# Self-attention weights: the turning of each rounded 128x1024 unit moved from TensorE to a transposing DMA

## The reference, cut to what matters

```python
sim  = einsum('bhid,bhjd->bhij', fq(q, dq, 128., 8), fq(k, dk, 128., 8)) * SCALE
attn = softmax(sim, axis=-1)
out  = einsum('bhij,bhjd->bhid', fq(attn, dw, 0., 8), fq(v, dv, 128., 8))
# fq(x, delta, zp, 8): clip(round(x / delta) + zp, 0, 255) minus zp, times delta
```

## Time and profile before

| | |
|---|---|
| median of 3 runs | 3900.94 us |
| profiled execution | 3903.09 us |
| its span, first to last instruction | 3901.3 us |
| busy: PE, PEld | 3174.2, 2210.8 us |
| busy: DVE, ACT, POOL | 2174.1, 1624.8, 1328.8 us |
| mean granted TensorE clock | 0.872 |
| DMA queue of SyncE | 509.14 MB, 35.8% of 16 engines |

### The profile page before, as it was taken

How to read it: one execution, slowest core, us unless ns; L and a number is a source line. 1 busy time by engine, 2 the same in 40 slices (tenths; PEclk the granted TensorE clock), 3 DMA queues, 4 the chain that set the end, 5 groups by cost and what they waited for, 6 DMA issues and landing times.

```text
span 3901.3 us, 50803 instructions
## 1 busy us (share of the span) xinstructions
PE 3174.2 (81%) x19712; PEld 2210.8 (57%) x19712; DVE 2174.1 (56%) x3559; ACT 1624.8 (42%) x2666; POOL 1328.8 (34%) x1025
## 2 busy tenths in 40 slices
PE   4445658789968799989967799889977799989989
PEld 4334433445656555655756655655756555655767
DVE  2324538667455567467445557467455567467431
ACT  3312136447422267357422257346422267357421
POOL 1231326344331234244241234244231244244231
PEclk8677765669988889999988879989988899999999
DMA  6873543312343322322344322322343322322334
GB/s 211 287 279 154 191 172 130 130 54 77 130 150 138 133 105 77 140 103 82 150 136 150 132 76 76 141 98 77 131 151 142 133 98 76 141 108 77 133 127 173
DMA packets 227694, 514.00 MB, mean 132 GB/s; under 512 B 96512, under 2 KB 113152, under 8 KB 205440
## 3 DMA queue, kind: packets, MB, share of 16 engines
q1 hardware_dynamic: 215040, 509.14, 35.8%
q10 hardware_dynamic: 12416, 1.62, 0.3%
HBM read 428.39 MB, written 82.31 MB: 131 GB/s over the span
## 4 chain that ended last, share of the span: by engine, by line
PE 62%; DVE 13%; issue 7%; POOL 6%; ACT 5%; DMA 4%; SPq 2%; ACTq 1%; POOLq 0%; DVEq 0%
PE psum L1461 17%; PE psum L1462 15%; PE psum L1463 15%; PE psum L1734 6%; PE psum L1725 6%; DVE mx L1341 2%; PE psum L1748 2%; DVE stats L1233 1%; POOL w1b L791 1%; DMA kept<-st_lo 1%; DVE w1T L1360 1%; POOL rstd L749 1%; DVE x L1229 1%; DVE den L1347 1%; ACT e L1062 1%
## 5 line engine op out<-in xcount | busy, mean ns | idle before, releaser
L791 POOL TENSOR_SCALAR w1b<-e,rec 128x1024 f16<-128x1024 f32 x512 | 572.8, 1119 | 903.9 <-DVE rec L1349 751.0
L1341 DVE TENSOR_REDUCE mx<-psum 128x1 f32<-128x1024 f32 x512 | 625.5, 1222 | 326.6 <-PE psum L1725 323.0
L1062 ACT ACTIVATE e<-psum,nb,scale 128x1024 f32<-128x1024 f32 x512 | 616.6, 1204 | 16.7
L1461 PE MATMUL psum<-h_hi,fw_hi 128*128 128x512 f32 x1024 | 463.7, 453 | 2.1 <-DVE h_lo L1152 2.1
L1734 PEld LDWEIGHTS psum<-ident,w1b 128*128 128x128 f16 x4096 | 264.6, 106 | 329.7 <-issue 261.7
L1725 PE MATMUL psum<-k,q 32*128 32x512 bf16 x1024 | 355.6, 432 | 103.3 <-ACT e L1062 83.2
L1463 PE MATMUL psum<-h_hi,fw_lo 128*128 128x512 f32 x1024 | 422.1, 412 | 0.0
L1462 PE MATMUL psum<-h_lo,fw_hi 128*128 128x512 f32 x1024 | 421.3, 411 | 0.0
L1734 PE MATMUL psum<-ident,w1b 128*128 128x128 f16 x4096 | 356.7, 237 | 72.1 <-DVE w1T L1360 60.7
L1360 DVE TENSOR_SCALAR w1T<-psum 128x1024 bf16<-128x1024 f16 x512 | 347.1, 678 | 44.2 <-PE psum L1734 42.8
L1461 PE MATMUL psum<-w_hi,ht_hi 128*128 128x512 f32 x640 | 268.8, 420 | 74.2 <-DVE e L1287 39.4
(11 more groups left out here) (165 smaller groups left out, 5763.5 us busy)
## 6 DMA issues: line engine op xcount, KB each, us to landing
fw_hi<-pieces SPq DMA_DIRECT2D x192, 512.0 KB, 3.2
fw_lo<-pieces SPq DMA_DIRECT2D x192, 512.0 KB, 4.2
w_hi<-kept SPq DMA_DIRECT2D x80, 1024.0 KB, 4.9
w_lo<-kept SPq DMA_DIRECT2D x80, 1024.0 KB, 7.4
fbias<-in_fside_Bx16xSxS SPq DMA_DIRECT2D x64, 256.0 KB, 4.1
prep_raw<-in_L_xattn_ff_w SPq DMA_DIRECT2D x12, 1024.0 KB, 8.1
pieces<-prep_hi SPq DMA_DIRECT2D x24, 512.0 KB, 3.6
pieces<-prep_lo SPq DMA_DIRECT2D x24, 512.0 KB, 5.6
```

Of the source, the lines that this page charges most:

```text
L791: pool.tensor_scalar(w1b[u % NH][:], e1[u % NE][:], rec1[:, u % 8:u % 8 + 1], HALF, ALU.mult, ALU.add).then_inc(w1_ready.sem, 1)
L1062: act.activation(e1[s % NE][:], psum[:, i:i + 2, :].rearrange("p i n -> p (i n)"), ACT.Exp, bias=nb1[:, s % 4:s % 4 + 1], scale=scale[:, 0:1],
L1341: dve.tensor_reduce(mx1[:, s % 4:s % 4 + 1], psum[:, i:i + 2, :].rearrange("p i n -> p (i n)"), AX, ALU.max).then_inc(maxed1.sem, 1)
L1461: pe.matmul(o, s_hi, m_hi, start=first, stop=False)
```

## The change

Each unit's weights are no longer turned by TensorE through PSUM. VectorE now works before the turning: in slot s, on unit s-4, it waits for GpSimd's buffer and subtracts 1024 and clips at 255 in that buffer, in place, fp16 read and bf16 written over the same bytes. SyncE then waits for VectorE and issues one transposing DMA of the whole unit, 128x1024 two-byte elements, from w1b into w1T. TensorE's product waits for the four DMAs of its group. GpSimd refills a w1b buffer when its DMA has landed; there are four of them instead of three. Bank 4 is not used in this stage any more. In SyncE's program the DMA of unit s-4 stands ahead of everything else of slot s. The second cross attention keeps its way over TensorE.

```diff
-LAG_T = 5
+LAG_W, LAG_T = 4, 5
...
-            fills += [("p1T", n, u, 4) for u in range(UNITS)]
...
-        NE, NH = 5, 3
+        NE, NH = 5, 4
...
+        w1_whole = signal("w1_whole", units)
+        w1T_landed = [signal(f"w1T_landed{i}", [(n, u) for n, u in units if u % 8 == i], 16) for i in range(8)]
...
+            def turn_unit(n, u):
+
+                sp.wait_ge(w1_whole.sem, w1_whole.at((n, u)))
+                if u >= 8 and u % 4 == 0:
+                    g = u // 4 - 2
+                    if g % 4 == 3:
+                        wait_filled(sp, ("a1", n, g // 4))
+                    else:
+                        sp.wait_ge(w1T_used.sem, w1T_used.at((n, g)))
+                sp.dma_start_transpose(w1T[u % 8][:], w1b[u % NH][:].bitcast(BF16)).then_inc(w1T_landed[u % 8].sem, 16)
...
                 for s in range(S_SLOTS):
+                    if 0 <= s - LAG_W < UNITS:
+                        turn_unit(n, s - LAG_W)
...
                 if u >= NH:
-                    wait_filled(pool, ("p1T", n, u - NH))
+                    last = w1T_landed[(u - NH) % 8]
+                    pool.wait_ge(last.sem, last.at((n, u - NH)))
...
-                    u = s - LAG_T
+                    u = s - LAG_W
                     if 0 <= u < UNITS:
-                        key = ("p1T", n, u)
-                        wait_filled(dve, key)
...
-                        emptied_bank(dve.tensor_scalar(w1T[u % 8][:].rearrange("p k q -> p (k q)"),
-                                                       bank(bank_of(key)).bitcast(FP16), -HALF, W_HIGH, ALU.add, ALU.min), key)
+                        dve.wait_ge(w1_ready.sem, w1_ready.at((n, u)))
+                        dve.tensor_scalar(w1b[u % NH][:].bitcast(BF16), w1b[u % NH][:], -HALF, W_HIGH, ALU.add, ALU.min
+                                          ).then_inc(w1_whole.sem, 1)
...
-                    u = s - LAG_T
-                    if 0 <= u < UNITS:
-                        key = ("p1T", n, u)
-                        pe.wait_ge(w1_ready.sem, w1_ready.at((n, u)))
-                        wait_empty(key)
-                        for k in range(KEYT):
-                            ins = pe.transpose(bank(bank_of(key)).bitcast(FP16)[:, k * P:k * P + P],
-                                               w1b[u % NH][:, k * P:k * P + P], ident16[:])
-                        done(ins, key)
...
                         if part == 0:
-                            wait_emptied(pe, ("p1T", n, 4 * g + 3))
+                            for h in range(4):
+                                landed = w1T_landed[(4 * g + h) % 8]
+                                pe.wait_ge(landed.sem, landed.at((n, 4 * g + h)))
```

## The result

The change made the kernel slower: 4069.43 us median of four runs (4043.07 to 4079.38) against 3900.58 for the kernel before; ratio 1.0431, 95% interval 1.0393 to 1.0468. The profiled execution's span is 4061.1 us against 3901.3, the mean granted clock 0.799 against 0.872.

A forecast was written before the change was run, and what follows sets the result against it. TensorE sets the pace in seven of eight self-attention stages. Each: -34 + 34 + 5 + 3 = +8 us, seven +56; first stage +14, clock +28: +98, giving 4000 us. Forecast's own range 3910 to 4130, whole range 3800 to 4350.

The forecast's parts named there:

- Rival 1: Turning's landing as short as the shortest rows, 2.7 us; product waits under 1 us a group; 3770 us; chance 25%.
- rival 3: TensorE's clock falls in every group after waits of 3 us or more, a stage under 0.8; 4250 us; chance 12%.
- Removed, 34 us a stage: TensorE's eight transposes per unit and its bank wait go, saving 34 us in each of seven later stages, 238 us.
- VectorE's step, 0.43 us: In-place step in SBUF takes 0.43 us, from 678 ns out of PSUM, and may wait for a running GpSimd instruction.
- The new wait, 2.6 us in each of 13 groups a stage: TensorE stands 2.6 us before each product group for the DMA, landing taken as 4.5 us: 34 us a stage.
- Pieces ahead of a turning, 5 us a stage: Piece loads issued just ahead of a group's last unit delay its turning on the DMA engines, 5 us a stage.
- SyncE's issue under 2.3 us: Each turning's issue on SyncE takes less than a slot, 2.3 us, so SyncE keeps up.
- The prediction's 3,900 us more: Under rival 2: eight single-tile DMA transposes one after another, 10.5 us a unit, some 3,900 us more; 4 in 100.
- rival 2: Throughput: turnings hold SyncE or the DMA engines longer than a slot, so every unit waits; 4080 to 4700 us; 18%.
- Buffers, nothing: GpSimd refilling w1b only after the landing costs nothing, hidden by its 100 us idle a stage.
- First stage, +14: First self-attention stage: 10 us saved, 10 us waits, and 14 us for turnings behind seven keeps of prepared weights: +14.
- The clock, +28: TensorE's clock drops after two or three long waits a stage, 1.7 us each: 4 us a stage, +28.

The follow-up runs named there:

- experiments 2 to 4: Experiment 2, experiment 3, and a further run: the changed kernel with the product one slot later, 3923.12 us, ratio 1.0061.
- experiments 3 and 6: Experiment 3, and the changed kernel with the product one slot later plus six GpSimd buffers (3926.44 us) or GpSimd freed of landing waits (3930.83 us).
- experiment 3: Changed kernel with DMAs reading a constant tile, so GpSimd need not wait for landings while the product still does: 4050.56 us, ratio 1.0408.
- experiment 2: Changed kernel with all 512 turning DMAs run from another tile and only SyncE checking landings, eight units later: 3802.17 us, ratio 0.9766.
- experiment 1: Changed kernel without its transposing DMAs, the product reading a constant tile and the attention's result left out: 3793.63 us, ratio 0.9758.

## Why the prediction was right, and where its terms were off

It said slower, 4000 us, 3910 to 4130 as the forecast's own range; 4069 is in it. That the product's wait would eat more than the turning's removal gives is shown. That the number fits is in good part luck: by the prediction's own signs two rivals were under way as well. Rival 1's landing of 2.8 us was there, and waits of 0.9 us a group in the seven later stages, under its limit of 1 us (1.3 over all eight); so was rival 3's clock under 0.8 (0.76 in the fourth stage). And TensorE's busy time, to go down by some 30 us a stage, went from 173 to 178 in the fourth. Step by step:

- **Removed, 34 us a stage.** Mis-sized: 16 (114 over seven stages). I took TensorE's weight loads and nearly all of the bank wait as pure gain. TensorE's busy time did fall by 184 us, but 70 of these went into longer stops, and its time at half clock rose by 124 us. I had written only that not all of the bank wait need go; what the faster TensorE would wait for next, the gelu stops, I did not subtract.
- **VectorE's step, 0.43 us.** Right: 416 ns median. The mean of 528 (497 in the fourth stage) is drawn up as expected; in the timeline one took 1.11 us, from 1773.90 to 1775.01, and ended 0.28 us after two GpSimd scalings (from 1772.40, 2.33 us together) were over. Inferred from that overlap; no run isolated it.
- **The new wait, 2.6 us in each of 13 groups a stage.** The place is right (experiments 2 to 4). The sizes are not: a typical landing is 2.8 us, not 4.5, so about half the groups do not wait at all; a quarter of the landings are over 4.1 and a tenth over 5.85. In place of 34 us a stage there are 69 waits of 2.3 us: 59.8 us in the first stage, some 15 in each of the others, 162 in all. Of the 102 us in the later stages, 40 end with a landing that took over 4.1 us and 47 with one that took under 3, so it is not only the late landings that are waited for. Rival 1 (2.7 us landings) had the median right and would have been 239 to 299 us too low: it has the same saving of 34 us a stage, and no term for the clock.
- **Pieces ahead of a turning, 5 us a stage (35).** The mechanism is right, its size too small: moving them gave 91 us, clock included. I gave only the transfer a price; the issue on SyncE is held too (2.79 us in place of 1.24). Over the whole run, turnings issued within 4 us behind another transfer (144 of them) landed after 5.15 us in the median, the others after 2.76.
- **SyncE's issue under 2.3 us.** Right: 1.235 us median (6.7 at worst); turnings overlap and the queue keeps up. Beside it stands the rule of the Trainium skill, Advanced Engine Details and Errata, section X-Bar Transpose (TRN2), that transposing DMAs are as fast as regular ones; the trace agrees in that 256 KB land in 2.7 us, the bias load's best.
- The Trainium skill, VectorE: DVE Perf Modes, section The three transpose paths, gives 1309 ns for one 128x128 tile by DMA. For eight one after another that would be an estimated 10.5 us; the trace differs, with 2.8 us for eight in one DMA. No run here turns a single tile. (The prediction's 3,900 us more, counted as it counts rival 2, would be some 3,800.)
- **Buffers, nothing.** Right for the seven later stages and the total (experiments 3 and 6), although GpSimd waits 142 us for landings; in the first stage it is not, see next.
- **First stage, +14.** It was +30; experiment 3 puts 20 of it on GpSimd's refill. The trace has seven such waits there, 38 us together, each for a turning issued behind the four stores of a prepared block: the one whole at 601.1 was issued at 603.5 and landed at 609.5. The place is what the prediction said of the keeps, the size is not.
- **The clock, +28.** The worst-sized term: 186 us, nearly seven times as much. I counted 1.7 us after each of two or three long stops a stage; the time at 1.2 GHz in the later stages is 783 us against 360 in experiment 2, and of it 556 against 61 us lie in the stretches of over 13 us. Rival 3 had the clock falling with the waits, but with longer waits and in every group.

For the seven stages I had 322 us on and 238 off, +84; it is 236 on and 114 off, +122. The total came near because the wait and the saving were too large and the clock too small.

No version beat the kernel before. The best complete one, two slots later, is 0.4% slower (3912.05 us, interval 0.2 to 0.7%), and even with no turning at all the kernel gains only 2.4% (experiment 1).

## What to carry to other kernels

Work taken off the engine that sets the pace is worth its duration only until the next thing that engine waits for: find that stop in the trace and subtract it before counting the gain. When a producer moves to a DMA, price the wait by the landing's spread and by what stands in front of it in the queue, and give it slack first: one slot of lag returned some 146 of 169 us here. Compare TensorE's busy time for the same instruction count between two runs, beside the granted clock; growth is the clock's part of the loss, the rest is stops. A small wait can cost more by the clock than by its own length.

## What the runs showed of the hardware

- A transposing DMA of 128x1024 two-byte elements issues in 1.235 us on SyncE and lands in 2.7 to 2.8 us when alone; right behind two 512 KB transfers it took 5.76. Transfers beside it slow a little (pieces 3.8 and 4.9 us in the changed kernel, 4.2 and 5.3 in experiment 2, against 3.2 and 4.2 before), at no cost in time in the later stages of experiment 2.
- The granted clock stayed at 1.2 GHz for 17 to 44 us at a time in the changed kernel, with TensorE busy for 89 to 100% of it. Adding 4096 transposes that do nothing made the kernel 49 us faster, at clock 0.852 in place of 0.799.
